# The last tile's last columns as a half and two quarters, with the last store on ScalarE's queue

## The reference

```
x = x + 0.5 * ffn(layernorm(x))
x = x + attention(layernorm(x))          # its own layer norm, cumulative sums over 256 tokens
x = x + 0.5 * ffn(layernorm(x))

def ffn(x):                              # 128 -> 512 -> 512 -> 512 -> 128, the same weights both times
    h = silu(x @ w1.T * s1) * (x @ w2.T * s2)
    h = gelu(h @ h1.T * s_h1)
    h = gelu(h @ h2.T * s_h2)
    return h @ w3.T * s3
```

## Time and profile before

| | |
|---|---|
| median of 3 runs | 376.67 us (376.67 to 377.38) |
| profiled execution | 376.7 us, its span 374.9 us |
| TensorE products busy | 368.0 us |
| VectorE, ScalarE busy | 321.9 us, 314.1 us |
| GpSimd busy | 52.6 us |
| TensorE clock | granted at 0.998 of full speed over the run |

### The profile page before, as it was taken

How to read it: one execution, slowest core, us unless ns; L and a number is a source line. 1 busy time by engine, 2 the same in 40 slices (tenths; PEclk the granted TensorE clock), 3 DMA queues, 4 the chain that set the end, 5 groups by cost and what they waited for, 6 DMA issues and landing times.

```text
span 374.9 us, 5278 instructions
## 1 busy us (share of the span) xinstructions
PE 368.0 (98%) x1662; PEld 291.9 (78%) x1662; DVE 321.9 (86%) x713; ACT 314.1 (84%) x549; POOL 52.6 (14%) x67
## 2 busy tenths in 40 slices
PE   7999999999999999999999999999999999999996
PEld 2678888787787877778788787778877778788885
DVE  5898787999999799999988999989799999976733
ACT  4999699989977999798699979967998998686763
POOL 3531101202101202201021120102101210020000
PEclk9999999999999999999999999999999999999999
DMA  7760000000000000000000000000000000000001
GB/s 246 277 265 1 2 0 0 1 2 1 0 2 0 1 2 2 2 0 1 2 0 1 2 1 28 2 28 1 2 29 0 0 30 1 30 1 28 2 0 58
DMA packets 4494, 9.81 MB, mean 26 GB/s; under 512 B 625, under 2 KB 1905, under 8 KB 4209
## 3 DMA queue, kind: packets, MB, share of 16 engines
q1 hardware_dynamic: 3744, 8.65, 6.3%
q10 hardware_dynamic: 720, 0.80, 0.6%
HBM read 7.35 MB, written 2.10 MB: 25 GB/s over the span
## 4 chain that ended last, share of the span: by engine, by line
PE 95%; DMA 2%; DVE 1%; SPq 1%; issue 0%; ACT 0%; ACTq 0%
PE hid_ps L449 60%; PE gate_ps L449 8%; PE y_ps L449 7%; PE up_ps L449 7%; PE xt_ps L462 3%; DMA x_sb<-x 2%; PE y_ps L462 2%; PE xt_ps L632 2%; PE xt_ps L629 2%; PE xt_ps L635 2%; PE up_ps L507 1%; PE gate_ps L507 1%; DVE gate L855 0%; PE xt_ps L449 0%; DVE xt_sb L924 0%
## 5 line engine op out<-in xcount | busy, mean ns | idle before, releaser
L449 PE MATMUL hid_ps<-act_hi,hi_h 128*128 128x512 f32 x480 | 195.6, 408 | 0.0
L449 PE MATMUL hid_ps<-act_lo,hi_h 128*128 128x512 f32 x480 | 186.8, 389 | 0.0
L877 DVE TENSOR_TENSOR act_lo<-full,act_hi 128x512 fp32r<-128x512 f32 x185 | 122.2, 683 | 26.8 <-ACT act_hi L708 24.3
L701 ACT ACTIVATE full<-hid_ps,vec 128x512 f32<-128x512 f32 x123 | 84.4, 686 | 34.9 <-PE hid_ps L449 31.2
L449 PEld LDWEIGHTS hid_ps<-act_hi,hi_h 128*128 128x128 f32 x480 | 90.1, 188 | 22.4 <-issue 4.1
L449 PEld LDWEIGHTS hid_ps<-act_lo,hi_h 128*128 128x128 f32 x480 | 90.2, 188 | 22.1 <-issue 4.3
L708 ACT ACTIVATE act_hi<-full 128x512 fp32r<-128x512 f32 x127 | 78.5, 630 | 2.3
L362 POOL TENSOR_TENSOR rstd<-veps,half 128x4 f32<-128x4 f32 x24 | 35.2, 1467 | 272.5 <-DVE veps L840 272.5
L855 DVE SCALAR_TENSOR_TENSOR gate<-tanh,gate_ps 128x512 f32<-128x512 f32 x60 | 40.6, 679 | 9.2 <-ACT tanh L684 8.6
L684 ACT ACTIVATE tanh<-gate_ps,s_half 128x512 f32<-128x512 f32 x60 | 40.8, 686 | 8.2 <-PE gate_ps L449 8.2
L867 DVE SCALAR_TENSOR_TENSOR full<-up_ps,s_half,gate 128x512 f32<-128x512 f32 x60 | 44.2, 742 | 0.9
(11 more groups left out here) (159 smaller groups left out, 397.8 us busy)
## 6 DMA issues: line engine op xcount, KB each, us to landing
xt_sb<-xt SPq DMA_DIRECT2D x1, 2048.0 KB, 10.9
out<-xt_sb SPq DMA_DIRECT2D x7, 256.0 KB, 2.0
x_sb<-x SPq DMA_DIRECT2D x1, 1536.0 KB, 6.6
raw_h<-h2t SPq DMA_DIRECT2D x4, 256.0 KB, 7.3
raw_h<-h1t SPq DMA_DIRECT2D x2, 256.0 KB, 5.9
raw_w<-w2t ACTq DMA_DIRECT2D x1, 256.0 KB, 4.0
raw_w<-w1t SPq DMA_DIRECT2D x1, 256.0 KB, 3.8
raw_h<-h1t ACTq DMA_DIRECT2D x1, 256.0 KB, 6.7
```

The lines of the kernel that those rows point to most:

```text
L449: mm = eng.matmul(ps, w, a, start=(first and n == 0), stop=(last and n == len(seq_) - 1))
L701: eng.activation(full23[m % 2][:, :], home23(n, T, m)[:, :], ACT.Gelu, scale=col("sh1" if n == 2 else "sh2", m)).then_inc(s_gelu[n], 1)
L877: eng.tensor_tensor(act_lo[a][:, m, :], full[m % 2][:, :], act_hi[a][:, m, :].bitcast(F32), ALU.subtract).then_inc(s_lo[n], 1)
```

## The change

The last tile's columns are cut at 256 and 384 instead of at 256 alone: a half and two quarters. Everything in the last step that was done for two halves is done for three pieces: the products of the last chunk (`last:p3.0` to `.2`), the gelu, the last layer and the addition. The third piece uses a quarter of the banks `up_ps[0]` and `up_ps[1]`. SP still stores the first two pieces. The third is stored by a DMA that ScalarE issues at the very end of its program.

```diff
 LAST_STEP = {
-    "PE": "... last:p4a last:p3.0 last:p3.1 last:p4b last:p4c.0 last:p4c.1",
+    "PE": "... last:p4a last:p3.0 last:p3.1 last:p3.2 last:p4b last:p4c.0 last:p4c.1 "
+          "last:p4c.2",
...
-        last_hid = [halves(hid_ps[1], 0), halves(gate_ps[0], 1)]
-        last_y = [halves(gate_ps[1], 0), halves(xt_ps, 1)]
+        LAST = (slice(0, TOK // 2), slice(TOK // 2, 3 * TOK // 4), slice(3 * TOK // 4, TOK))
+        last_hid = [bank_[:, c] for bank_, c in zip((hid_ps[1], gate_ps[0], up_ps[0]), LAST)]
+        last_y = [bank_[:, c] for bank_, c in zip((gate_ps[1], xt_ps, up_ps[1]), LAST)]
...
-            for h in range(2):
+            for h in (0, 1):
                 eng.wait_ge(s_last_x, h + 1)
-                eng.dma_start(halves(out[:, (NT - 1) * TOK:], h), halves(xt_tile(NT - 1), h)).then_inc(s_out, 16)
-            eng.wait_ge(s_out, 16 * (NT + 1))
+                eng.dma_start(out[:, (NT - 1) * TOK:][:, LAST[h]], xt_tile(NT - 1)[:, LAST[h]]).then_inc(s_out, 16)
+            eng.wait_ge(s_out, 16 * (NT + 2))
...
             def last_p4(T, ks, general):
-                for h in range(2):
+                for h in range(3):
                     products(last_y[h], [("w3", k, 0, *last_layer(3, T, k, h)) for k in ks], None, general,
                              first=(ks[0] == 0), last=False)
...
             schedule("ACT", emit, "rest")
+            eng.wait_ge(s_last_x, 3)
+            eng.dma_start(out[:, (NT - 1) * TOK:][:, LAST[2]], xt_tile(NT - 1)[:, LAST[2]]).then_inc(s_out, 16)
```

More of the change, by code:

```diff
@@ L90 @@
 LAST_STEP = {
-    "PE": "p2.0 p2.1 p2.2 p2.3 p4 p3.0 p3.1 p3.2 last:p4a last:p3.0 last:p3.1 last:p4b last:p4c.0 last:p4c.1",
+    "PE": "p2.0 p2.1 p2.2 p2.3 p4 p3.0 p3.1 p3.2 last:p4a last:p3.0 last:p3.1 last:p3.2 last:p4b last:p4c.0 last:p4c.1 "
+          "last:p4c.2",
     "ACT": "gelu2.0 gelu2.1 high2.0 high2.1 gelu2.2 high2.2 gelu2.3 high2.3 gelu3.0 high3.0 gelu3.1 high3.1 "
-           "gelu3.2 high3.2 last:gelu.0 last:gelu.1",
-    "DVE": "low2.0 low2.1 low2.2 low2.3 low3.0 low3.1 dt low3.2 last:dt.0 last:dt.1",
+           "gelu3.2 high3.2 last:gelu.0 last:gelu.1 last:gelu.2",
+    "DVE": "low2.0 low2.1 low2.2 low2.3 low3.0 low3.1 dt low3.2 last:dt.0 last:dt.1 last:dt.2",
 }
@@ L532, in last_layer @@
                 hi, lo = layer(n, T, k, wait=(h == 0))
-                return (halves(hi[0], h), hi[1]), (halves(lo[0], h), lo[1])
+                return (hi[0][:, LAST[h]], hi[1]), (lo[0][:, LAST[h]], lo[1])
             def last_p3(T, h, general):
@@ L546, in last_p4_end @@
                 eng.wait_ge(s_last_gelu, h + 1)
-                eng.matmul(last_y[h], wblk(raw, "w3", MC - 1, 0), halves(full23[(MC - 1) % 2], h), start=False,
+                eng.matmul(last_y[h], wblk(raw, "w3", MC - 1, 0), full23[(MC - 1) % 2][:, LAST[h]], start=False,
                            stop=True).then_inc(s_last_p4, 1)
@@ L718, in last_gelu @@
                     eng.wait_ge(s_lo[3], MC * T + MC - 2)
-                eng.activation(halves(full23[(MC - 1) % 2], h), last_hid[h], ACT.Gelu,
+                eng.activation(full23[(MC - 1) % 2][:, LAST[h]], last_hid[h], ACT.Gelu,
                                scale=col("sh2", MC - 1)).then_inc(s_last_gelu, 1)
@@ L922, in emit @@
                     eng.wait_ge(s_last_p4, chunk + 1)
-                    xt_half = halves(xt_tile(t), chunk)
+                    xt_half = xt_tile(t)[:, LAST[chunk]]
                     eng.scalar_tensor_tensor(xt_half, last_y[chunk], s3_half[:, 0:1], xt_half, ALU.mult,
```

## The result

| | before | after |
|---|---|---|
| median, 20 runs each | 376.71 us | 377.75 us |
| ratio, 95% interval | | 1.0024 (1.0018 to 1.0030) |
| profiled execution | 376.7 us, span 374.9 us | 377.56 us, span 375.7 us |

The change makes the kernel slower by 0.24%, 0.9 us (0.7 to 1.1). The forecast was 378.0 us.

A forecast was written before the change was run, and what follows sets the result against it. TensorE's own instruction stream was taken to bound the kernel, then additions and stores. +1.40 for products and -0.05 for the tail gave +1.35 on span 374.9, 376.25; with 1.8 outside the span, 378.0 us, range 377.3 to 378.9.

The forecast's parts named there:

- The products: TensorE before the first fp32 pass: twenty-eight products of 128 columns replace fourteen of 256, +1.40 us, bounds +1.32 to +1.68.
- The rival in which loads hide: TensorE's weight loads are queued ahead, gap between 0.067 and 0.11 us, total 376.8 to 377.4 us; chance 0.13.
- The last products and the additions: After the first fp32 pass: TensorE's products end 1.04 us behind its start (before 1.03), VectorE's additions 1.63 (before 1.55), +0.08.
- The tail: Everything after the first fp32 pass starts, additions, stores and program end: -0.05 us, bounds -0.15 and +0.15.
- The branch begins 0.2 before the first pass of the last product.: TensorE's branch over the general code copy starts 0.46 us after the first fp32 pass starts; TensorE done at 3.9.
- The landing gains 0.15.: Last store's landing, against 3.90 us behind the first fp32 pass's start before, comes 0.15 us earlier.
- a sign of being wrong: Prediction is wrong if the gap is near 0.07, or branch or a store's landing differs by more than 0.5.
- both last stores now fall into it and land at t + 3.9.: If the instruction fetch stalled SP's second issue, both last stores meet it, landing 3.9 us after the first fp32 pass starts.
- Faster: Rival at the last store: ScalarE's queue avoids SP's 0.59 us stall with half the bytes, 376.3 us; chance 0.03.
- The tail gets worse: Rival at the end: fetch or third store delays the last landing, or branch waits again, 378.7 to 379.0 us; chance 0.12.

The follow-up runs named there:

- the split into +0.82 and +0.57: Two runs: kernel before with only `last:p3.1` in two groups of 128 columns, 377.58 us; changed kernel with the third layer's last chunk back in halves, 377.33 us.
- the runs without the copy: Second copy of TensorE's last program part left out: kernel before 376.25 us, changed kernel 377.78 us, kernel before with second half's store on ScalarE 376.41 us.
- the repeat on ScalarE: Kernel before, halves kept, second half's store issued by ScalarE instead of SP, run a second time: 376.74 us, ratio 0.9993 (0.9984 to 1.0002).
- third-layer run: Changed kernel with the third layer's last chunk back in two halves of 256 columns, all the rest as changed: 377.33 us, ratio 1.0012.

## Why the prediction was right

**The products: right.** The step was 28 x 0.11 - 14 x 0.120 = +1.40, measured +1.38; the gap taken from lines 625 and 626 was 0.11, measured 0.111. The rival in which loads hide (0.067 to 0.11) is refuted by the timeline, and the split into +0.82 and +0.57 shows that the cost goes with the number of narrow products. That the 0.11 is the weight load and not another fixed cost of a product rests on the row behind the wait and on line 626; every product of this kernel has its own load (1662 of each), so no run separates the two. The 81 ns of the Trainium skill (TensorE: Matmul & The Clock Gate, "Back-to-back issue gap") would have given +0.59; the trace shows 111 ns with float32r, and the measurement decides.

**The last products and the additions: right in kind.** First fp32 pass to last product's end was to be 1.04 and is 372.51 + 0.39 - 371.81 = 1.09, since the first pass stood behind a narrow product and took 0.05 longer. The last addition ends at 1.68 in place of the forecast 1.63.

**The tail: right in sign, too small.** The term of -0.05 for the whole tail, with bounds of -0.15 and +0.15, measured -0.39, outside its bounds. This term is why the total was 1.35 and not the measured 0.9 to 1.0. Two parts of it failed:

- "The branch begins 0.2 before the first pass of the last product." It begins when the last gelu is done, and not when the last product is issued. Before, `gelu` ended at 370.82 and the branch began at 370.9. After, the rows are these, from the timeline of ScalarE:

```profile
370.43 0.37 ACT L721 ACTIVATE full<-gate_ps,vec 128x128 f32<-128x128 f32 x1 [0.37 <-PE gate_ps L451]
371.32 0.37 ACT L721 ACTIVATE full<-up_ps,vec 128x128 f32<-128x128 f32 x1 [0.53 <-PE up_ps L451]
```

  The last gelu ends at 371.69 and the branch begins at 371.7, ahead of the first fp32 pass at 371.81. The sequencer went on to the branch while products were still to run; the last thing it waited for was this gelu. With a wait for the additions put in its way the branch began at 372.2, when the last of them was done (371.63 + 0.48 = 372.11 in that run). So TensorE was done at 375.2, 3.4 behind the first pass and not 3.9, and did not hold the end.
- "The landing gains 0.15." It gained 0.39: t + 3.50 for t + 3.89 (SP goes on at 375.3 and 374.5), t being the start of the first fp32 pass. The last store landed 1.8 after its issue for 2.3, and its issue began 0.14 later behind t. That 0.5 is already the difference that the prediction named as a sign of being wrong. Its working was loose too: with SP's quarter at t + 3.70 as the floor, the middle up to t + 3.96 is t + 3.83, a gain of 0.07. The gain comes from the fetch: in the runs without the copy the tails are 3.8 and 3.9. These are the slices in which it begins (16 KB in 0.2 us are 82 GB/s), before and after, from the view by stretches:

```profile
371.80:372.00 0.20, 0.00 (x0) 0.00 (x0) 0.20 (x1) 0.00 (x0) 0.00 (x0) 1.00 0.29 82
```

```profile
372.60:372.80 0.20, 0.20 (x3) 0.11 (x1) 0.20 (x1) 0.00 (x0) 0.00 (x0) 1.00 0.29 82
```

  SP's second issue begins at 372.21 before and at 373.01 + 1.01 - 0.63 = 373.39 after: 0.56 before the fetch ends and then 0.26. It took 0.634 instead of 0.922. ScalarE's store was issued from 373.53 on, at the very end of the fetch (373.65), and its bytes moved from 374.4 on, clear of it. What the quarter's fewer bytes bring is little, 1.8 against 1.8 to 1.9 where no fetch runs.

The prediction had seen this fetch and drawn the opposite from it: "both last stores now fall into it and land at t + 3.9." That followed from the branch, which it placed at t + 0.46. The branch began at t - 0.1, so the fetch ended at t + 1.84, where it had ended at t + 2.14 before, while the last store was issued at t + 1.72 in place of t + 1.58.

So the gain in the tail is not what the cut was forecast to bring, but relief from a disturbance that the old order ran into, and it is luck. Without the copy the old order has that relief too, and the change shows its full cost: 1.0024 against 0.9979, 0.45%, or 1.5 us between the medians. That is TensorE's 1.38 and a tail of 3.9 for 3.8.

**The rivals.** "Faster" needed a gap under 0.08: refuted. "The tail gets worse" did not happen in the changed kernel's profile; the run with only `last:p3.1` cut (tail 4.5) and the repeat on ScalarE (4.5) show that it can, when an issue or a landing falls behind the fetch.

**What stays open.** No run settles whether ScalarE's queue alone is worth 0.06% to the kernel before, nor why the fetch stalls the second issue of a queue and spares the first. A version with all products in halves and only additions and stores in quarters was not tried.

## What to carry to other kernels

Before cutting the last tile finer, look at how far apart products start: where each has its own weight load, a product of 128 columns costs nearly as much as one of 256 here, so a cut down to 256 columns is nearly free (0.120 against half of 0.227) and the next one doubles the bill. Price a tail by what it is made of: here additions and stores have fixed parts (0.34 for half the width of 0.48; 1.8 for 64 KB against 1.9 for 128 KB), so a third piece wins almost nothing back. And look for what else runs in the last three microseconds: an instruction fetch behind a long branch can hold up the last store (0.922 for 0.378 to issue it, 2.3 for 1.9 to land it).

## What the runs showed of the hardware that was not expected

A branch over a long piece of code at the end of TensorE's program costs other engines something. It takes 3.3 to 4.0 us and brings a 16 KB instruction fetch, of 0.93 us before and 1.2 us in the third-layer run (5.0% of 16 engines over 1.5 us). While that runs, the second store of SP's queue waits in its issue: it took 0.922 before and 0.634 in the changed kernel, but 0.378 and 0.433 where the fetch was gone and 0.377 where it came later. The first store of a queue was issued in 0.33 to 0.36 throughout. A fetch that comes while a store is in flight instead delays one sixteenth of it: the landing then took 3.8 for 1.9. The Trainium skill (Runtime: NRT & Kernel Launch, "Instruction fetch mechanics") says that a taken branch whose target is outside the window forces a DMA fetch of the target page before execution can go on; the trace agrees: the fetch is there with the branch and gone without it. It adds that this fetch delays stores of another engine. Removing it took 0.21% (0.11 to 0.30) off the kernel before.
